# The shared expert's second half and the router: their order in one gated block, on one core

## Chip, cores, metric

One core of one Trainium2 chip. The metric is the device time of one execution in microseconds, as the median of several. TensorE does matrix products, VectorE and ScalarE elementwise work, GpSimd (POOL in the profile) elementwise work more slowly, SyncE (SP) issues DMAs.

## The reference

A gated block on x (8 x 56 tokens of 256): cross attention of 16 heads to 8 contexts of 1500 rows, with fake int8 quantisation on both outer products, then a mixture of 16 experts, two a token, and a shared expert. Only the second part is touched:

```python
x = x + tanh(g_xattn[0]) * xattn(layernorm(x), ctx_2048, ...)
xt = layernorm(x).reshape(-1, D)                      # T = 448 tokens, D = 256
logits = xt @ gate_w.T                                # E = 16
scores = sqrt(softplus(logits))
_, idx = top_k(scores + gate_b, 2)
w = take_along_axis(scores, idx, 1); w = w / w.sum(1, keepdims=True)
pos = position of each (token, choice) among its expert's; valid = pos < CAP   # CAP = 128
buf = zeros((E, CAP, D)).at[e, posc].add(x_pairs)
h = silu(buf @ W1.T) * (buf @ W3.T)                   # I = 176 hidden rows
y = combine(h @ W2.T, w * valid)
shared = (silu(xt @ Ws1.T) * (xt @ Ws3.T)) @ Ws2.T
out = x + tanh(g_ffn[0]) * (y + shared)
```

## The kernel before, in words

Every engine has one list of instructions, written out by hand in its own block; engines meet by semaphores only, and `need(engine, name, n)` is a wait for a count. An engine works its list in order, so where a step stands in the list matters as much as what it waits for.

Attention takes the first 300 us (64 slots, `pe_slot`, `act_slot`, `dve_slot`). Then the attention's output is quantised, projected (L1217) and added (L871), and normalised again (`normalise`, L691, into `xn`, tiles 0 to 2 and then tile 3; tiles are of 112 tokens). The standard deviations come from GpSimd (L445).

From there the second part. Numbers of float32 are carried as two float16 halves: a high half, which ScalarE rounds, and a low half, the difference. A product of two such numbers is three float16 products (`split3`). ScalarE makes the high halves: `xT16[:, 0]` from the turned tokens (L597), `x16[:, :, 0]` from the tokens (L608), `hT[:, 0]` from the shared expert's hidden rows (L611), `w2T` and `w13T` from the weights (`w2_hi` L517, `w13_hi` L523). VectorE makes the low halves of the turned tokens (L876, L878), of the shared hidden rows (L927), and of `w13T` (`w13_lo`, L842). GpSimd makes the low half of `x16` (L448) and of `w2T` (`w2_lo`: a scaling, L436, which waits only for the weight's load, then a subtraction, L439, which waits for `w2_hi`).

TensorE turns the tokens (L1233, L1237), forms the logits in bank 3 (L1243), then the shared expert's gates and ups of four tiles (L1254, banks 2, 4, 5, 7). VectorE copies the logits (L883) and computes softplus from them by a series (L885 to L898) with ScalarE's exp and sqrt (L599, L606), then the two selections (the loop at L912, five steps L914 to L918 each). Between them stand the shared expert's products: `hidden(p)` (L903, L905) makes gate times up of tiles 2p and 2p+1. TensorE turns these into `h_bank` (L1261), ScalarE and VectorE split them (L611, L927), and TensorE multiplies by the shared second weights (L1276), tiles 0 and 1 (p = 0) and 2 and 3 (p = 1). Between the two p stand the places: from `sel16` (the choices, cast at L924) TensorE counts each choice's place (L1268), VectorE finishes `place` (L937, L938).

`place` is turned (L1333), copied by ScalarE (L645) and sent by SP to memory and back as rows (L339 to L343); SP's later weight loads stand behind these. VectorE also compares it to slot numbers (`select`, L946). With this 0/1 matrix TensorE gathers an expert's tokens (`gather`, L1286), ScalarE copies them (`tokens_hi`, L618), TensorE forms gates and ups (`gates_and_ups`, L1303, logged at L1018 in `split3`), ScalarE and VectorE the hidden rows (L628, L973, L977), TensorE turns them (`turn_hidden`, L1310), forms results (L1318, also logged at L1018) and adds them to the tokens in banks 0 and 1 (`add`, L1327). The loop over the 16 experts runs this one expert ahead.

Of the kernel before, what the change touches and what calls it, by code (L numbers as in the profile page):

```python
# [99 lines left out]
def program(nc, x, ctx, cols, rows, gate, wq, wkv, wp, W13, W2, out):  # L100
    stack = ExitStack()
    with stack:
# [129 lines left out]
        def bank16(b):  # L232
# [8 lines left out]
            shared_gu shared_tanh shared_h shared_ht shared_hh shared_hl shared_y xh_done xl_done x16_ready place_turned place_copied place_out place_in0 place_in1 w2_scaled  # L241
# [26 lines left out]
        g_bank = (2, 4, 5, 7)  # L268
        h_bank = (3, 6)
        place_bank = 2  # L270
# [81 lines left out]
        def _(gp):  # L352
# [94 lines left out]
            gp.wait_ge(s["act_post"], 4)  # L447
            gp.tensor_tensor(x16[:, :, 1], xn[:], x16[:, :, 0], ALU.subtract).then_inc(s["x16_ready"], 1)  # L448
# [6 lines left out]
        def _(act):  # L455
# [136 lines left out]
            act.activation(xqT[:, :, 3 * TP:T], bank16(4)[:, 0:NH * TP].rearrange("p (h t) -> p h t", h=NH), ACT.Copy).then_inc(s["oqc_done"], 1)  # L592
            turned = (PS[:, 0:NH, 0:3 * TP], PS[:, 5, 0:NH * TP].rearrange("p (h t) -> p h t", h=NH))
            for k, part in enumerate((slice(0, 3 * TP), slice(3 * TP, T))):
                act.wait_ge(s["lnt_done"], k + 1)
                act.activation(xT[:, :, part], turned[k], ACT.Copy).then_inc(s["lnc_done"], 1)
                act.activation(xT16[:, 0, :, part], turned[k], ACT.Copy).then_inc(s["xh_done"], 1)  # L597
            act.wait_ge(s["dve_post"], 3)
# [9 lines left out]
            act.activation(x16[:, :, 0], xn[:], ACT.Copy).then_inc(s["act_post"], 1)  # L608
            for p in range(2):
                act.wait_ge(s["shared_ht"], p + 1)  # L610
                act.activation(hT[:, 0, p, :], PS[0:IH, h_bank[p], 0:4 * TP], ACT.Copy).then_inc(s["shared_hh"], 1)  # L611
            w2_hi(1)
            w13_hi(1)
# [28 lines left out]

            act.wait_ge(s["shared_y"], 2)
            act.wait_ge(s["place_turned"], 1)
            act.activation(placeT[:], PS[0:E * TT, turn_bank, 0:TP], ACT.Copy).then_inc(s["place_copied"], 1)  # L645
            tokens_hi(0)
# [8 lines left out]
        def _(dve):  # L655
# [217 lines left out]
            for k, part in enumerate(groups):  # L873
                normalise(x1, xn, range(part.start, part.stop), 2 + k).then_inc(s["ln_done"], 1)
            dve.wait_ge(s["xh_done"], 1)
# [4 lines left out]

            logit, e_, z, z2, acc, a, b_, c_ = (r[0], r[1], r[2], r[3], r[4], r[5], r[6], r[7])
# [30 lines left out]
            for k, oh in enumerate((e_, z)):  # L912

                one(dve.tensor_reduce(rs[0][:], bias[:], AX.X, ALU.max))  # L914
                one(dve.tensor_tensor(a[:], bias[:], rs[0][:].unsqueeze(2).to_broadcast([TP, TT, E]), ALU.is_ge))
                one(dve.tensor_tensor(a[:], a[:], rank[:], ALU.mult))
                one(dve.tensor_reduce(rs[0][:], a[:], AX.X, ALU.max))
                one(dve.tensor_tensor(oh[:], a[:], rs[0][:].unsqueeze(2).to_broadcast([TP, TT, E]), ALU.is_equal))  # L918
                if k == 0:
                    one(dve.scalar_tensor_tensor(bias[:], oh[:], -3e38, bias[:], ALU.mult, ALU.add))  # L920
                    hidden(1)
                if k == 1:
                    one(dve.tensor_tensor(c_[:], e_[:], z[:], ALU.add))
                    post(dve.tensor_copy(sel16[:], c_[:]))  # L924

                dve.wait_ge(s["shared_hh"], k + 1)
                dve.tensor_tensor(hT[:, 1, k, :], PS[0:IH, h_bank[k], 0:4 * TP], hT[:, 0, k, :], ALU.subtract).then_inc(s["shared_hl"], 1)  # L927

            one(dve.tensor_tensor(a[:], sc[:], c_[:], ALU.mult))
# [9 lines left out]
            dve.wait_ge(s["act_post"], 3)  # L939
            d.did(dve.tensor_scalar(tgf[:], tg[:, 1:2], 1.0 / FS, None, ALU.mult))  # L940
            d.settle()

# [52 lines left out]
            select(0)  # L995
            select(1)
            w13_lo(1)
            slot_weights(0)
            hidden_rows(0)
# [11 lines left out]
        def _(pe):  # L1011
# [239 lines left out]
            for t in range(TT):  # L1251
                if t == 3:
                    need(pe, "dve_post", 1)
                split3(PS[0:TP, g_bank[t], 0:2 * I], lambda a, h: xT16[:, a, h, t * TP:(t + 1) * TP],  # L1254
                       lambda a, h: w13T[0][:, a, h, :]).then_inc(s["shared_gu"], 1)
            for p in range(2):
                pe.wait_ge(s["shared_h"], 2 * p + 2)
                pe.wait_ge(s["dve_post"], 2)
# [4 lines left out]
            for p in range(2):  # L1263
                if p == 1:
                    pe.wait_ge(s["dve_post"], 4)
                    for t in range(TT):
                        for k in range(t + 1):
                            last = mm(PS[0:TP, place_bank, t * E:(t + 1) * E], (before16 if k == t else ones16)[:], sel16[:, k, :],  # L1268
                                      start=k == 0, stop=k == t)
                    last.then_inc(s["pe_post"], 1)  # L1270
# [7 lines left out]
                last.then_inc(s["shared_y"], 1)  # L1278
            def gather(e):
# [53 lines left out]
            tp(PS[0:E * TT, turn_bank, 0:TP], place[:], ident[0:TP, 0:TP]).then_inc(s["place_turned"], 1)  # L1333
            gather(0)
            weigh_slots(0)
            gates_and_ups(0)
            for e in range(E):
# [63 lines left out]
```

## Time and profile before

| | us |
|---|---|
| median of 3 runs | 416.7 (414.03, 416.7, 418.24) |
| the profiled execution | 412.87 |
| its span, first to last instruction | 411.0 |
| mean granted clock of TensorE | 0.948 |

| engine | busy us | share |
|---|---|---|
| TensorE | 361.2 | 88% |
| VectorE | 304.3 | 74% |
| ScalarE | 250.6 | 61% |
| GpSimd | 124.2 | 30% |

Every time in a row is from the start of the span. A timeline row has the start, the duration, the engine, the line and the operation with its shapes; in brackets the engine's idle time before it and the instruction that ended it. A row may stand for several instructions (x2). The granted clock is a share of full speed, 2.4 GHz: 0.50 is 1.2 GHz.

### The profile page before, as it was taken

The numbers are of one execution on the slowest core, as the hardware profiler recorded it, in microseconds if no ns is written. First come the engines' busy times: TensorE is split into PE (matmuls) and PEld (weight loads), VectorE is DVE, ScalarE is ACT, GpSimd is POOL, SyncE is SP. The second block draws the span as 40 slices with busy tenths as digits, with TensorE's granted clock in tenths as the row PEclk, the third lists the DMA queues.
The fourth block names the chain that finished last, engine by engine and source line by source line (L and its number), as shares of the span: only waits on it lengthen the run. The fifth ranks groups of instructions, "written<-read, shape, count | busy, mean of one in ns | idle before, by whom it ended". The sixth has DMA issues, their size and how long they took to land.

```text
span 411.0 us, 14015 instructions
## 1 busy us (share of the span) xinstructions
PE 361.2 (88%) x5793; PEld 270.3 (66%) x5793; DVE 304.3 (74%) x656; ACT 250.6 (61%) x412; POOL 124.2 (30%) x116
## 2 busy tenths in 40 slices
PE   0996899999999998998999999997853789999993
PEld 0672468568658676766856866874642677888882
DVE  3889885866775775776586676667787786999993
ACT  3574567767776686676776766566532425766661
POOL 6151642222132022122222200010101063777870
PEclk9999799999999999999999999999895757999998
DMA  8969983663474284186163146560000008645001
GB/s 252 192 166 207 208 202 78 106 170 106 76 165 100 81 171 123 51 147 181 54 101 92 39 73 119 146 186 31 3 2 2 0 2 275 196 133 155 8 0 45
DMA packets 34512, 45.65 MB, mean 111 GB/s; under 512 B 3995, under 2 KB 30299, under 8 KB 34323
## 3 DMA queue, kind: packets, MB, share of 16 engines
q1 hardware_dynamic: 33395, 43.74, 44.5%
q0 software_dynamic: 640, 0.78, 1.0%
q8 instruction: 46, 0.75, 0.8%
q10 hardware_dynamic: 416, 0.26, 0.3%
q14 instruction: 15, 0.12, 0.1%
HBM read 25.08 MB, written 0.47 MB: 62 GB/s over the span
## 4 chain that ended last, share of the span: by engine, by line
PE 77%; DVE 13%; issue 4%; ACT 2%; POOL 1%; DMA 1%; DVEq 0%; ACTq 0%; POOLq 0%
PE PS L1018 36%; PE PS L1061 9%; PE PS L1084 9%; PE PS L1095 9%; PE PS L1327 4%; PE PS L1286 3%; DVE mx L777 2%; PE PS L1071 2%; PE PS L1310 2%; DMA x_in<-x 1%; PE PS L1243 1%; DVE KN L726 1%; DVE st L680 1%; PE PS L1276 1%; DVE mtop L781 1%
## 5 line engine op out<-in xcount | busy, mean ns | idle before, releaser
L777 DVE TENSOR_REDUCE mx<-PS 112x1 f32<-112x500 f32 (+1 forms) x128 | 114.4, 933 | 58.5 <-PE PS L1061 58.5
L491 ACT ACTIVATE PT_all<-PS 128x1344 f32<-128x1344 f32 x64 | 82.5, 1289 | 9.2 <-PE PS L1084 9.1
L1018 PE MATMUL PS<-cT,wkvT 128*128 128x500 f16 x288 | 71.5, 385 | 17.7 <-POOL zero L392 11.3
L1018 PE MATMUL PS<-wkvT,cT 128*125 128x256 f16 x576 | 72.8, 278 | 0.5 <-issue 0.5
L1018 PEld LDWEIGHTS PS<-wkvT,cT 128*125 128x125 f16 x576 | 64.9, 139 | 5.9 <-issue 1.1
L385 POOL TENSOR_TENSOR cT<-c_in,cT 128x1000 f16<-128x1000 f32 x18 | 37.5, 2084 | 87.3 <-ACT cT L469 87.3
L1018 PEld LDWEIGHTS PS<-cT,wkvT 128*128 128x128 f16 x288 | 27.5, 99 | 50.5 <-POOL zero L392 11.2
L476 ACT ACTIVATE KN<-PS,col_in 128x500 f16<-128x500 f32 x48 | 32.5, 677 | 40.7 <-PE PS L1018 40.7
L1061 PE MATMUL PS<-arena,QC 96*112 96x500 f16 x192 | 53.1, 384 | 3.1 <-issue 3.1
L1084 PE MATMUL PS<-QC,arena 98*128 98x112 f16 x768 | 49.2, 214 | 3.3 <-ACT QC L511 3.2
L483 ACT ACTIVATE V<-PS 125x512 f32<-125x512 f32 x48 | 28.7, 597 | 31.4 <-PE PS L1018 31.4
L1084 PEld LDWEIGHTS PS<-QC,arena 98*128 98x128 f16 x768 | 41.5, 99 | 9.6 <-ACT QC L511 4.1
L1095 PE MATMUL PS<-PT_all,V 125*17 125x56 f32 x3072 | 45.7, 215 | 1.7 <-ACT PT_all L491 1.6
L726 DVE SCALAR_TENSOR_TENSOR KN<-PS,col_in,KN 128x500 f16<-128x500 f32 x48 | 35.3, 736 | 12.0 <-ACT KN L476 11.2
L1095 PEld LDWEIGHTS PS<-PT_all,V 125*17 125x17 f32 x3072 | 40.3, 99 | 4.1 <-ACT PT_all L491 3.0
L439 POOL TENSOR_TENSOR arena<-arena 88x512 f16<-88x512 f32 x17 | 24.8, 1459 | 34.8 <-ACT arena L517 34.7
L1018 PE MATMUL PS<-arena 88*128 88x256 f16 (+2 forms) x216 | 33.5, 307 | 0.8 <-ACT arena L618 0.7
L409 POOL TENSOR_TENSOR QC<-q,par 96x448 f16<-96x448 f16 x16 | 15.2, 952 | 57.4 <-PE PS L1084 55.6
L1018 PEld LDWEIGHTS PS<-arena 88*128 88x128 f16 (+2 forms) x216 | 22.6, 106 | 9.2 <-issue 1.2
L1061 PEld LDWEIGHTS PS<-arena,QC 96*112 96x112 f16 x192 | 20.5, 133 | 9.9 <-issue 4.2
L469 ACT ACTIVATE cT<-c_in 128x1000 f16<-128x1000 f32 x24 | 24.9, 1036 | 1.8 <-DMA c_in<-ctx 1.4
L1071 PEld LDWEIGHTS PS<-ident,nm 112*2 112x2 f16 x64 | 5.1, 79 | 22.2 <-issue 17.0
(205 smaller groups left out, 449.7 us busy)
## 6 DMA issues: line engine op xcount, KB each, us to landing
arena<-KN SPq DMA_DIRECT2D x144, 125.0 KB, 3.6
c_in<-ctx SPq DMA_DIRECT2D x24, 500.0 KB, 4.6
cT<-W SPq DMA_DIRECT2D x11, 352.0 KB
c_in<-W SPq DMA_DIRECT2D x6, 352.0 KB
cT<-W SPq DMA_DIRECT2D x11, 176.0 KB
arena<-place_far SPq DMA_DIRECT2D x1, 1568.0 KB, 10.3
c_in<-W SPq DMA_DIRECT2D x6, 176.0 KB
PT_all<-L_xattn_wkv SPq DMA_DIRECT2D x1, 512.0 KB, 6.1
```

The costliest lines, as they stand in the source:

```text
L385: gp.tensor_tensor(cT[:, n % 2, 1, :, c * CW:(c + 1) * CW], c_in[:, :, c * CW:(c + 1) * CW], cT[:, n % 2, 0, :, c * CW:(c + 1) * CW], ALU. ...
L439: gp.tensor_tensor(w2T[j % 2][:, 1], w2_s, w2T[j % 2][:, 0], ALU.subtract).then_inc(s["w2l_done"], 1)
L469: act.activation(cT[:, n % 2, 0, :, c * CW:(c + 1) * CW], c_in[:, :, c * CW:(c + 1) * CW], ACT.Copy).then_inc(s["th_done"], 1)
L476: act.activation(KN[:, oh, c, 0, :], PS[:, BANK["K", n, u], 0:CW], ACT.Identity, bias=bk_c[:, oh:oh + 1]).then_inc(s["kh_done"], 1)
L483: act.activation(V[:, n % 2, 2 * v:2 * v + 2, :, 0:DH], PS[0:KP, BANK["V", n, v], :].rearrange("p (t h j) -> p t h j", t=2, h=H), ACT.Copy ...
L491: act.activation(PT_all[:, u % 4, :].rearrange("p (c k) -> p c k", c=CH), PS[:, 3:6, 0:4 * TP], ACT.Exp, scale=SCORE).then_inc(s["exp_done ...
L726: dve.scalar_tensor_tensor(KN[:, oh, c, 1, :], PS[:, BANK["K", n, u], 0:CW], bk_c[:, oh:oh + 1], KN[:, oh, c, 0, :], ALU.add, ALU.subtract ...
L777: dve.tensor_reduce(mx[:, u % 2, k:k + 1], PS[0:TP, k:1 + k * (CH - 1), 0:CW], AX.XY, ALU.max).then_inc(s["red_done"], 1)
L1018: ins = mm(out_, w(a, h), x_(b, h), start=first and k == 0, stop=last and k == len(todo) - 1)
L1061: mm(PS[0:TP, c, 0:CW], QC[0:QR, b % 2, i * TP:(i + 1) * TP], KS[0:QR, b % 2, i, c * CW:(c + 1) * CW], start=True, stop=True).then_inc(s[" ...
L1084: last = mm(PS[:, 3 + t // 4, (t % 4) * TP:(t % 4 + 1) * TP], KS[0:QR + 2, b % 2, i, t * KP:t * KP + 128], QC[0:QR + 2, b % 2, i * TP:(i + ...
L1095: last = mm(PS[32 * j:32 * j + VW, bank, 0:S], V[:, b % 2, t, 4 * hg + j, :], PT[:, (2 * g + j // 2) % 4, t * TP + (j % 2) * S:t * TP + (j ...
```

## The change

- VectorE: `hidden(1)` leaves the loop of the two selections and comes between `select(0)` and `select(1)`. The low halves of the shared hidden rows leave the loop as `shared_lo(p)`: 0 comes behind both selections, 1 behind `slot_weights(0)`. The scale `tgf` comes behind that. `w13_lo(1)` moves from behind `select(1)` to ahead of the low halves of the turned tokens. The low half of `x16` moves from GpSimd to VectorE, ahead of the logits' copy.
- ScalarE: `w2_hi(1)` and `w13_hi(1)` move ahead of the second layer norm's work; the high half of `x16` is made in two parts around the turned tokens' copies, with a semaphore of its own. The shared hidden rows' copy 0 stays, copy 1 comes behind `tokens_hi(0)`; the copy of `place` no longer waits for `shared_y`; that wait stands ahead of `w2_hi(2)`.
- TensorE: turn 0, places, results 0; then the turn of `place`, gather and slot weights of expert 0, turn 1, gates and ups of expert 0, results 1.
- Banks: the shared gates use 2, 6, 4, 3 (the fourth waits for the logits' copy), both turns use bank 5, `place` is turned into bank 6.

```diff
@@ -238,7 +238,7 @@
             oq_done oqt_done oqc_done proj_done ln_done lnt_done lnc_done
-            shared_gu shared_tanh shared_h shared_ht shared_hh shared_hl shared_y xh_done xl_done x16_ready place_turned place_copied place_out place_in0 place_in1 w2_scaled
+            shared_gu shared_tanh shared_h shared_ht shared_hh shared_hl shared_y xh_done xl_done x16h_done x16_ready place_turned place_copied place_out place_in0 place_in1 w2_scaled
             w2h_done w2l_done w13h_done w13l_done
@@ -265,9 +265,9 @@
         proj_at = ((2, 0), (2, D), (1, 0), (3, 0))
-        g_bank = (2, 4, 5, 7)
-        h_bank = (3, 6)
-        place_bank = 2
+        g_bank = (2, 6, 4, 3)
+        h_bank = (5, 5)
+        place_bank, place_t_bank = 2, 6
         gather_bank, gu_bank, turn_bank, y_bank, sum_bank = 2, 3, 4, 5, 7
@@ -444,8 +444,6 @@
-            gp.wait_ge(s["act_post"], 4)
-            gp.tensor_tensor(x16[:, :, 1], xn[:], x16[:, :, 0], ALU.subtract).then_inc(s["x16_ready"], 1)
             for j in range(1, E + 1):
@@ -590,11 +588,21 @@
             act.activation(xqT[:, :, 3 * TP:T], bank16(4)[:, 0:NH * TP].rearrange("p (h t) -> p h t", h=NH), ACT.Copy).then_inc(s["oqc_done"], 1)
+            w2_hi(1)
+            w13_hi(1)
+            def x16_hi(k, part):
+                act.wait_ge(s["ln_done"], k + 1)
+                act.activation(x16[:, part, 0], xn[:, part], ACT.Copy).then_inc(s["x16h_done"], 1)
+            x16_hi(0, groups[0])
             turned = (PS[:, 0:NH, 0:3 * TP], PS[:, 5, 0:NH * TP].rearrange("p (h t) -> p h t", h=NH))
...
                 act.activation(xT16[:, 0, :, part], turned[k], ACT.Copy).then_inc(s["xh_done"], 1)
+            x16_hi(1, groups[1])
             act.wait_ge(s["dve_post"], 3)
@@ -605,12 +613,13 @@
             act.activation(tg[:, 1:2], gx[:, 1:2], ACT.Tanh).then_inc(s["act_post"], 1)
-            act.activation(x16[:, :, 0], xn[:], ACT.Copy).then_inc(s["act_post"], 1)
-            for p in range(2):
+            def shared_hi(p):
                 act.wait_ge(s["shared_ht"], p + 1)
                 act.activation(hT[:, 0, p, :], PS[0:IH, h_bank[p], 0:4 * TP], ACT.Copy).then_inc(s["shared_hh"], 1)
-            w2_hi(1)
-            w13_hi(1)
+            shared_hi(0)
@@ -640,10 +649,11 @@
+            act.wait_ge(s["place_turned"], 1)
+            act.activation(placeT[:], PS[0:E * TT, place_t_bank, 0:TP], ACT.Copy).then_inc(s["place_copied"], 1)
+            tokens_hi(0)
+            shared_hi(1)
             act.wait_ge(s["shared_y"], 2)
-            act.wait_ge(s["place_turned"], 1)
-            act.activation(placeT[:], PS[0:E * TT, turn_bank, 0:TP], ACT.Copy).then_inc(s["place_copied"], 1)
-            tokens_hi(0)
             w2_hi(2)
@@ -872,12 +882,15 @@
                 normalise(x1, xn, range(part.start, part.stop), 2 + k).then_inc(s["ln_done"], 1)
+            w13_lo(1)
             dve.wait_ge(s["xh_done"], 1)
...
+            dve.wait_ge(s["x16h_done"], 2)
+            dve.tensor_tensor(x16[:, :, 1], xn[:], x16[:, :, 0], ALU.subtract).then_inc(s["x16_ready"], 1)
             logit, e_, z, z2, acc, a, b_, c_ = (r[0], r[1], r[2], r[3], r[4], r[5], r[6], r[7])
@@ -918,14 +931,16 @@
                     one(dve.scalar_tensor_tensor(bias[:], oh[:], -3e38, bias[:], ALU.mult, ALU.add))
-                    hidden(1)
                 if k == 1:
...
-                dve.wait_ge(s["shared_hh"], k + 1)
-                dve.tensor_tensor(hT[:, 1, k, :], PS[0:IH, h_bank[k], 0:4 * TP], hT[:, 0, k, :], ALU.subtract).then_inc(s["shared_hl"], 1)
+            def shared_lo(p):
+                dve.wait_ge(s["shared_hh"], p + 1)
+                dve.tensor_tensor(hT[:, 1, p, :], PS[0:IH, h_bank[p], 0:4 * TP], hT[:, 0, p, :], ALU.subtract).then_inc(s["shared_hl"], 1)
+            shared_lo(0)
             one(dve.tensor_tensor(a[:], sc[:], c_[:], ALU.mult))
@@ -936,10 +951,6 @@
             post(dve.tensor_scalar(place[:].rearrange("p (e t) -> p t e", t=TT), b_[:], -1.0, None, ALU.add))
-            dve.wait_ge(s["act_post"], 3)
-            d.did(dve.tensor_scalar(tgf[:], tg[:, 1:2], 1.0 / FS, None, ALU.mult))
-            d.settle()
             def select(e):
@@ -993,9 +1004,13 @@
             select(0)
+            hidden(1)
             select(1)
-            w13_lo(1)
             slot_weights(0)
+            shared_lo(1)
+            dve.wait_ge(s["act_post"], 3)
+            d.did(dve.tensor_scalar(tgf[:], tg[:, 1:2], 1.0 / FS, None, ALU.mult))
+            d.settle()
             hidden_rows(0)
@@ -1250,24 +1265,21 @@
                 if t == 3:
-                    need(pe, "dve_post", 1)
+                    need(pe, "dve_post", 2)
                 split3(PS[0:TP, g_bank[t], 0:2 * I], lambda a, h: xT16[:, a, h, t * TP:(t + 1) * TP],
                        lambda a, h: w13T[0][:, a, h, :]).then_inc(s["shared_gu"], 1)
-            for p in range(2):
+            def turn_shared(p):
                 pe.wait_ge(s["shared_h"], 2 * p + 2)
-                pe.wait_ge(s["dve_post"], 2)
+                need(pe, "shared_hl", p)
                 for k in range(2):
...
                 last.then_inc(s["shared_ht"], 1)
-            for p in range(2):
-                if p == 1:
-                    pe.wait_ge(s["dve_post"], 4)
-                    for t in range(TT):
-                        for k in range(t + 1):
-                            last = mm(PS[0:TP, place_bank, t * E:(t + 1) * E], (before16 if k == t else ones16)[:], sel16[:, k, :],
-                                      start=k == 0, stop=k == t)
-                    last.then_inc(s["pe_post"], 1)
+            def shared_results(p):
                 pe.wait_ge(s["shared_hl"], p + 1)
@@ -1276,6 +1288,15 @@
                 last.then_inc(s["shared_y"], 1)
+            turn_shared(0)
+            pe.wait_ge(s["dve_post"], 4)
+            for t in range(TT):
+                for k in range(t + 1):
+                    last = mm(PS[0:TP, place_bank, t * E:(t + 1) * E], (before16 if k == t else ones16)[:], sel16[:, k, :],
+                              start=k == 0, stop=k == t)
+            last.then_inc(s["pe_post"], 1)
+            shared_results(0)
             def gather(e):
@@ -1330,10 +1351,12 @@
             pe.wait_ge(s["dve_post"], 5)
-            tp(PS[0:E * TT, turn_bank, 0:TP], place[:], ident[0:TP, 0:TP]).then_inc(s["place_turned"], 1)
+            tp(PS[0:E * TT, place_t_bank, 0:TP], place[:], ident[0:TP, 0:TP]).then_inc(s["place_turned"], 1)
             gather(0)
             weigh_slots(0)
+            turn_shared(1)
             gates_and_ups(0)
+            shared_results(1)
             for e in range(E):
```

## Rows read from the trace of the kernel before

**Rows 1.** The chain of waits, 332 to 360 us (start, us, what).
```profile
332.95 0.20 DVE sel L924
333.20 1.11 PE PS L1268 x10
...
337.13 1.72 PE PS L1286 x16
...
343.33 0.49 PE PS L1310 x2
...
359.95 1.55 PE PS L1018 x12
```

**Rows 2.** TensorE's timeline, where it had been idle.
```profile
329.80 0.58 PE L1261 MATMUL PS<-ident,PT_all 112*88 112x112 f32 x4 [2.57 <-DVE PT_all L905]
330.33 2.69 PE L1276 MATMUL PS<-arena 88*112 88x256 f16 x12
...
339.62 1.92 PE L1018 MATMUL PS<-arena 128*128 128x352 f16 x6 [0.69 <-ACT arena L618]
```

**Rows 3.** Windows: us, PE, PEld, DVE, ACT, POOL busy, PEclk, DMA share, GB/s.
```profile
330.50:331.00 0.50, 0.50 (x4) 0.50 (x4) 0.50 (x1) 0.50 (x2) 0.50 (x1) 0.50 0.00 0
...
344.00:344.50 0.50, 0.50 (x4) 0.29 (x5) 0.23 (x1) 0.24 (x1) 0.00 (x0) 0.86 1.07 426
```

**Rows 4.** VectorE's timeline, 317 to 343 us.
```profile
317.96 0.86 DVE L876 TENSOR_TENSOR arena<-qT,arena 128x672 f16<-128x672 f32 x1 [2.54 <-ACT arena L597]
318.73 0.38 DVE L878 TENSOR_TENSOR arena<-qT,arena 128x224 f16<-128x224 f32 x1
320.56 0.22 DVE L883 COPY r<-PS 112x64 f32<-112x64 f32 x1 [1.44 <-PE PS L1243]
...
327.01 0.23 DVE L915 TENSOR_TENSOR r<-r,rs 112x64 f32<-112x64 f32 x1
...
328.30 0.34 DVE L903 SCALAR_TENSOR_TENSOR PT_all<-PT_all,PS 112x176 f32<-112x176 f32 x1
...
329.67 0.61 DVE L927 TENSOR_TENSOR arena<-PS,arena 88x448 f16<-88x448 f32 x1
...
330.43 1.02 DVE L915 TENSOR_TENSOR r<-r,rs 112x64 f32<-112x64 f32 x1
331.49 0.66 DVE L916 TENSOR_TENSOR r<-r,rank 112x64 f32<-112x64 f32 x1
...
335.66 0.22 DVE L938 TENSOR_SCALAR place<-r 112x64 f32<-112x64 f32 x1
...
342.30 0.40 DVE L977 SCALAR_TENSOR_TENSOR PT_all<-PS,slot_w,PT_all 128x176 f32<-128x176 f32 x1
```

**Rows 5.** GpSimd's timeline, 314 to 334 us.
```profile
314.21 0.65 POOL L445 TENSOR_TENSOR rstd<-var,mhalf 112x1 f32<-112x1 f32 x1 [0.82 <-DVE var L686]
329.25 2.12 POOL L448 TENSOR_TENSOR arena<-xn,arena 112x1024 f16<-112x1024 f32 x1 [14.39 <-ACT arena L608]
331.46 1.49 POOL L436 TENSOR_SCALAR arena<-c_in 88x512 f32<-88x512 f32 x1
333.04 1.15 POOL L439 TENSOR_TENSOR arena<-arena 88x512 f16<-88x512 f32 x1
```

**Rows 6.** ScalarE's timeline, 316 to 342 us.
```profile
316.57 0.73 ACT L596 ACTIVATE qT<-PS 128x672 f32<-128x672 f32 x1 [7.36 <-PE PS L1233]
...
328.12 1.06 ACT L608 ACTIVATE arena<-xn 112x1024 f16<-112x1024 f32 x1
...
339.37 0.62 ACT L517 ACTIVATE arena<-cT 88x512 f16<-88x512 f32 x1
341.57 0.32 ACT L628 ACTIVATE PT_all<-PS 128x176 f32<-128x176 f32 x1 [1.58 <-PE PS L1018]
```

**Rows 7.** Timelines of VectorE and GpSimd in the attention, at 48 us.
```profile
48.13 2.20 DVE L786 SCALAR_TENSOR_TENSOR nm<-mtop,nm 112x1 f16<-112x1 f32 x1
...
47.96 2.35 POOL L426 TENSOR_TENSOR x<-x_in,row_in 112x1024 f32<-112x1024 f32 x1
```

## The prediction

> **What bounds the kernel now.** I read the chain of waits first, from the second layer norm (314 us) to the end, then the timeline of each engine in 314 to 350, then windows of half a microsecond for the granted clock. The chain shows two regimes. From 343.33, where the first expert's hidden rows are turned [rows 1], the chain lies on TensorE without a break, expert after expert; the last row of [rows 1] is one of 16 equal pieces. Whatever the change gives must therefore be there at 343.33: behind it nothing is edited, and TensorE's list for an expert is the same. Ahead of it, from the logits to the choice's cast (332.95), the chain runs through VectorE's router [rows 1]. From 333.20 on it is TensorE again: places, shared results, gather, gates, one behind the other [rows 1].
>
> So the question is TensorE's gaps between 327.2 (end of the first turn of the shared hidden rows) and 343.33. Its timeline has three: 2.57 us ahead of the second turn, 0.18 ahead of the places, 0.69 ahead of the first expert's gates, which wait for ScalarE's copy of the gathered tokens [rows 2]. Sum 3.44. The work between them is only reordered by the change. It can win these 3.44 and no more, unless the clock moves. The clock is at its lower level, 1.2 GHz, from about 330.5 (0.50 granted; TensorE had mostly idled since 327.2) until about 344.0, where it goes back to 2.4 GHz (0.86 granted in that half microsecond) [rows 3].
>
> **The change, part by part.**
>
> Router without interruptions. Out of VectorE's queue between the two selections go hidden(1), two pairs, and the first difference of the shared hidden rows: 328.30 to 330.28, 1.98 us [rows 4]. The router's steps also lose their stalls: the same line 915 took 0.23 us in the first selection and 1.02 in the second, with the neighbour 916 at 0.66, while GpSimd made the tokens' low half (329.25, 2.12 us) and started the next weight [rows 4, 5]. With that subtraction gone from GpSimd and the weight's work done long before, both take 0.23: 0.79 + 0.43 = 1.2. The cast moves from 332.95 to 329.75, ends at 329.95.
>
> Tokens' low half on VectorE. New ahead of the logits' copy: one subtraction of 1024 columns. Two subtractions of this form took 0.86 us at 672 columns and 0.38 at 224 [rows 4], 1.07 ns a column, so 1.24 us. It starts behind line 878 (318.73 + 0.38 = 319.11) and ends at 320.35; the logits' copy started at 320.56 after 1.44 us idle [rows 4]. It is hidden with 0.2 to spare. Its ScalarE half is split in two; the whole took 1.06 [rows 6], so the part of 768 columns some 0.8, in ScalarE's wait ahead of the turned tokens, which ends at 316.57 [rows 6] and of which some 1.4 us are left when the first three tiles are normalised (VectorE's wait before line 876 begins at 317.96 - 2.54 = 315.42 with the fourth, a piece of 0.3 later); the part of 256 ends at about 318.8, ahead of 319.11. w2_hi(1) and w13_hi(1), 0.6 and 0.8 us each by the like rows, go into the same wait, which was 7.36 long [rows 6]. If that cover were gone they would delay the turned tokens by 1.4 at most.
>
> w13_lo(1), 0.9 us, goes from a place where VectorE waits anyway to that wait of 2.54 us between the normalised tokens and 317.96 [rows 4]: nothing.
>
> GpSimd's earlier work. With w2h_done raised early, GpSimd runs w2_lo(1) and the scaling of w2_lo(2) right behind the second rstd (314.21 + 0.65 = 314.86): 1.49 + 1.15 + 1.49 and two pauses of 0.09 [rows 5], until 319.2. That is beside VectorE's three subtractions, all with two inputs in SBUF, and such steps are what was held. Bounds: nothing, if they miss each other (GpSimd's own subtraction would end at 317.7, before 317.96); and two holds of the size of line 916's (0.43 each) less the 0.2 to spare, some 0.6. I take 0.2, nearer the lower end, since 916 was the only thing a scaling held. The cast then ends at 330.15.
>
> A rule here speaks against the change. The row: on another stretch a VectorE step of one column took 2.20 us beside a GpSimd sum of 2.35 [rows 7]. The Trainium skill, "SBUF — State Buffer", section "SBUF: two separate sides", says that the pair of ports is an exclusive lock: a VectorE step with two SBUF inputs and a GpSimd step that reads SBUF take turns, each for its whole length. The row of 2.20 agrees. But line 916 was free after 0.66 beside a scaling of 1.49 that had started 0.03 before it [rows 4, 5], so for scalings the trace disagrees. By the rule the sum would come out slower; by the rows it does not (second rival).
>
> TensorE, with the durations of this trace. Idle from 327.2 to 330.2: 3.0 us, the lull ends later than before. Places 1.11 [rows 1], to 331.3. shared_results(0) 2.69 [rows 2], to 334.0. It needs shared_hl 1, which follows the cast by 0.6: there. Meanwhile VectorE needed 2.73 us from the end of the cast to the place numbers (333.15 to 335.88 [rows 1, 4]); now at most that, 332.9, then select(0), 0.65. Turn of places 0.2, gather(0) 1.72 [rows 1], slot weights 0.1: 336.0. The second turn, 0.58 [rows 2], to 336.6, stands where the 0.69 gap was: ScalarE's copy of the tokens (0.6) runs beside it. hidden(1) is done by 335.2. Gates 1.92 [rows 2], to 338.5; shared_results(1) 2.69, to 341.2; its shared_hl 2 is there by 337.8. Then gather(1), 1.72 and 0.1, to 343.0.
>
> New wait: ScalarE waits for shared_y 2 at 341.2 with w2_hi(2), hidden_tanh(0) and all that follows queued behind it. 0.62 for w2_hi(2), then 1.13 from the tanh's start to the end of VectorE's product (341.57 to 342.70 [rows 4, 6]): the hidden rows are ready at 342.95. So the turn is released by both at about 342.95 to 343.0 instead of 343.33. The gap sum agrees: 3.44 out, 3.0 in, 0.4 won. GpSimd's w2_lo(2) slips by 1.8 us behind w2_hi(2), to 342.7, five microseconds before results(1) wants it. SP's three DMAs of the places go 3 us sooner, and the weight loads behind them in its queue too; nobody waited for them.
>
> Clock. From 330.2 to 343 TensorE has no gap now, so I expect the return to 2.4 GHz sooner than 344.0. If it comes near 341 it only speeds gather(1), which then waits for the hidden rows (342.95), and the next gates a little: 0.2. Sum: 0.4 + 0.2 = 0.6 faster.
>
> The profiled execution took 412.87 (span 411.0), 3.8 below the median of the three runs, 416.7 (414.03 to 418.24). Forecast 412.3 for a like execution, so 416.1 for the median. The forecast's own spread is 0.1 to 1.0 faster.
>
> **Rivals.**
>
> *One*: the clock returns ahead of the first gates, at about 336.6. The warm price of gates and results together is 1.55 for six matmuls of 352 columns and six of 256 [rows 1], by columns 0.90 and 0.65; twelve of 256 then 1.30. Gates to 337.5, shared_results(1) from 337.8 (its difference) to 339.1, hidden rows at 340.85: 2.5 faster, 414.2. For: no gap ahead of it since 330.2. Against: here TensorE worked from 333.2 to 338.9 without one and the clock stayed at 0.50. Chance 0.25.
>
> *Two*, slower: the shared ports take full turns. w13_lo(1) waits for the scaling (316.45) and runs to 317.35, GpSimd's subtraction to 318.5, line 876 to 319.35, the next scaling to 320.85, line 878 to 321.2, the new subtraction to 322.45. The logits' copy is 1.9 late, not 0.2, and the router, the lull and all behind it with it: -0.6 + 1.7 = 1.1 slower, 417.8. It decides from a delay of 0.8 on. For: the 2.20 and 1.02 rows. Against: the 0.66. Chance 0.12. (It is what the sentence of the Trainium skill's page "SBUF — State Buffer" told above would make of this kernel.)
>
> *Three*: all 3.2 us of the router reach the end, 413.5. That needs TensorE not to be full behind the cast; it is, but for 0.87. Chance 0.07.
>
> *Four*: the longer quiet (327.2 to 331.3 with only small matmuls, 2.57 idle before) lowers the clock in executions where it now survives. Price, cold against half: gates 1.0, two shared results 2.8, two gathers 1.7: 5.5, so 4.9 slower, 421.6. Against: in this trace it falls already. Chance 0.04; 0.02 is for what I have not seen.
>
> **How the numbers follow.** The forecast has 0.5. About 1%, 4.2 us, is what a measurement of this kernel can tell from no change. None of the cases but the fourth moves that far; what is left is the spread of the median itself, some 2 us by the three runs. Rivals one and three are 1.7 and 1.0 us from the bound: a quarter of their 0.32, and 0.04 of the rest, give faster 0.12. Slower is rival four and a little of two: 0.06. Within 1%: 0.82. Range: 412.6 to 418.4, from below rival three to above rival two.
>
> **What would show it.** Right: line 915 at 0.23 twice; the cast 9.2 us behind the logits' copy (12.4 before); TensorE idle 3 us ahead of the places and hardly at all between them and the first turn of hidden rows; experts as far apart as before. The logits' copy right behind the new subtraction, with steps 876 and 878 longer than 0.86 and 0.38, would show the ports. Wrong: an idle stretch of TensorE of over 0.5 us behind gather(1), a clock that stays at 0.50 beyond 344, or one that falls in other places.

## The result and the profile after

17 runs: median 414.09 us (409.93 to 417.18), before 416.88 (414.03 to 418.54) in the same rounds. The ratio is 0.992, 95% interval 0.989 to 0.995. The changed kernel again in a later batch, 12 runs, gave 0.9996 (0.9955 to 1.0036): e12 below. The two intervals lie side by side and do not overlap (0.9948 against 0.9955). So: faster by 0 to 1%, inside the forecast's 1%, and the time lies in the range. The ratios leave out executions more than 1.5% above the fastest of the same kernel; the profiled ones of the change, of e4 and of e5 are such, which is one more reason to compare kernels by a stretch of their traces, as follows.

The profiled execution of the changed kernel took 416.15 us, more than the 412.87 of before. All of that lies ahead of the normalisation. VectorE's normalisation, the last step that both kernels do alike, starts at 314.05 before and at 320.48 after. Only two of the moved ScalarE steps stand ahead of it (`w2_hi(1)`, `w13_hi(1)`), and they did not delay it: in both kernels it starts 5.19 us behind the start of ScalarE's last copy of the attention's turned output. From it to the logits' copy both need 6.51 us; and from the third expert's turn of hidden rows to the end both need 60.4. In all fourteen traces of this study that last figure is 60.38 to 60.41, and the first ranges from 313.66 to 320.48. Most of what differs from run to run is made in the attention. So I compare kernels by **the stretch**: from the logits' copy to the third turn. It is 30.08 us before (320.56 to 350.64, [rows 4] for its start) and 27.01 after (326.99 to 354.00). Its ends, and the normalisation, in VectorE's and TensorE's timelines, before and then after:

```profile
314.05 1.37 DVE L691 TENSOR_SCALAR xn<-x,mv,rstd 112x256 f32<-112x256 f32 x4
350.64 0.42 PE L1310 MATMUL PS<-ident,PT_all 128*88 128x128 f32 x2
```

```profile
320.48 1.66 DVE L701 TENSOR_SCALAR xn<-x,mv,rstd 112x256 f32<-112x256 f32 x4
354.00 0.42 PE L1331 MATMUL PS<-ident,PT_all 128*88 128x128 f32 x2
```

VectorE's timeline after. Lines 887, 889, 896, 928 and 936 are 876, 878, 883, 915 and 924 of [rows 1, 4]:

```profile
324.38 1.14 DVE L887 TENSOR_TENSOR arena<-qT,arena 128x672 f16<-128x672 f32 x1 [1.44 <-ACT arena L604]
325.44 0.38 DVE L889 TENSOR_TENSOR arena<-qT,arena 128x224 f16<-128x224 f32 x1
325.74 1.21 DVE L893 TENSOR_TENSOR arena<-xn,arena 112x1024 f16<-112x1024 f32 x1
326.99 0.22 DVE L896 COPY r<-PS 112x64 f32<-112x64 f32 x1
...
335.08 0.22 DVE L928 TENSOR_TENSOR r<-r,rs 112x64 f32<-112x64 f32 x1
335.34 0.22 DVE L929 TENSOR_TENSOR r<-r,rank 112x64 f32<-112x64 f32 x1
...
336.37 0.19 DVE L936 CAST sel<-r 112x64 f16<-112x64 f32 x1
...
338.61 0.22 DVE L953 TENSOR_SCALAR place<-r 112x64 f32<-112x64 f32 x1
```

The cast comes 9.38 us behind the logits' copy (12.39 before; forecast 9.2). The selection's steps take 0.22 each where they took 1.02 and 0.66. The new subtraction took 1.21 and ended at 326.95, when TensorE's logits ended too: hidden, with nothing to spare. GpSimd's early work shows in the first row, 1.14 for 0.86.

TensorE's timeline after, to set beside [rows 2]:

```profile
336.61 0.22 PE L1296 MATMUL PS<-sel,before 112*112 112x16 f16 x1 [2.95 <-DVE sel L936]
...
337.15 2.56 PE L1288 MATMUL PS<-arena 88*112 88x256 f16 x12
339.50 0.39 PE L1354 MATMUL PS<-ident,place 112*64 112x112 f32 x1
339.69 1.61 PE L1307 MATMUL PS<-arena 112*128 112x128 f16 x16
...
342.08 1.05 PE L1033 MATMUL PS<-arena 128*128 128x352 f16 x6 [0.27 <-ACT arena L627]
343.09 1.52 PE L1288 MATMUL PS<-arena 88*112 88x256 f16 x12
344.45 1.06 PE L1307 MATMUL PS<-arena 112*128 112x128 f16 x16
345.34 0.24 PE L1315 MATMUL PS<-wt,arena 112*128 112x2 f16 x4
346.41 0.42 PE L1331 MATMUL PS<-ident,PT_all 128*88 128x128 f32 x2 [0.83 <-DVE PT_all L988]
347.38 1.73 PE L1033 MATMUL PS<-arena 128*128 128x352 f16 x12 [0.55 <-DVE arena L852]
```

Two rows of before that [rows 2] does not have:

```profile
333.20 0.26 PE L1268 MATMUL PS<-sel,before 112*112 112x16 f16 x1 [0.18 <-DVE sel L924]
334.16 2.79 PE L1276 MATMUL PS<-arena 88*112 88x256 f16 x12
```

The gap ahead of the places is 2.95, as worked out (3.0). But the first gates take 1.05 where they took 1.92, the second shared results 1.52 instead of 2.79, and TensorE then stands idle twice, 0.83 and 0.55 us, for work that stands behind ScalarE's wait for `shared_y`. The windows say why (the columns are those of [rows 3]):

```profile
337.00:337.50 0.50, 0.50 (x9) 0.50 (x8) 0.44 (x3) 0.00 (x0) 0.00 (x0) 0.93 0.00 0
337.50:338.00 0.50, 0.50 (x4) 0.50 (x3) 0.42 (x3) 0.00 (x0) 0.00 (x0) 0.50 0.00 0
340.50:341.00 0.50, 0.50 (x9) 0.50 (x7) 0.48 (x2) 0.00 (x0) 0.00 (x0) 0.65 0.00 0
341.00:341.50 0.50, 0.50 (x13) 0.50 (x11) 0.50 (x2) 0.16 (x1) 0.00 (x0) 1.00 0.10 21
```

The clock fell to 1.2 GHz at 337.4 and was back at 340.8: low for 3.4 us of the stretch. Before, it was low from 330.5 to 344.1, 13.7 us [rows 3]. So the trace after is the case of my first rival: the clock is back ahead of the first gates (342.08).

### The profile page after: what moved, and what is told of

It is laid out like the page before. It is cut to its first block, busy times and chain, and to the rows that moved or that the text cites. A ratio compares the mean times of both kernels' runs of the same rounds, so it can differ in the third digit from the quotient of the medians.

```text
span 414.4 us, 14014 instructions
## 1 busy us (share of the span) xinstructions
PE 359.3 (87%) x5793; PEld 268.6 (65%) x5793; DVE 306.6 (74%) x657; ACT 250.8 (61%) x413; POOL 122.3 (30%) x115
## 4 chain that ended last, share of the span: by engine, by line
PE 76%; DVE 14%; issue 3%; ACT 2%; POOL 1%; DMA 1%; DVEq 0%; ACTq 0%; POOLq 0%
PE PS L1033 36%; PE PS L1076 9%; PE PS L1110 9%; PE PS L1099 9%; PE PS L1348 4%; PE PS L1307 3%; PE PS L1086 2%; DVE mx L787 2%; DVE mtop L791 2%; PE PS L1331 1%; DMA x_in<-x 1%; PE PS L1288 1%; DVE KN L736 1%; PE PS L1258 1%; DVE st L690 1%
## 5 line engine op out<-in xcount | busy, mean ns | idle before, releaser
L1033 PE MATMUL PS<-cT,wkvT 128*128 128x500 f16 x288 | 72.8, 390 | 22.1 <-POOL rank L393 11.3
L1033 PE MATMUL PS<-wkvT,cT 128*125 128x256 f16 x576 | 74.0, 281 | 0.0
L1033 PEld LDWEIGHTS PS<-wkvT,cT 128*125 128x125 f16 x576 | 66.1, 141 | 5.3 <-issue 0.5
L1110 PE MATMUL PS<-PT_all,V 125*17 125x56 f32 x3072 | 46.7, 218 | 1.6 <-ACT PT_all L489 1.6
L736 DVE SCALAR_TENSOR_TENSOR KN<-PS,col_in,KN 128x500 f16<-128x500 f32 x48 | 35.3, 737 | 14.6 <-ACT KN L474 13.9
L1110 PEld LDWEIGHTS PS<-PT_all,V 125*17 125x17 f32 x3072 | 41.3, 101 | 4.1 <-ACT PT_all L489 4.0
```

Source lines behind the costliest of these rows:

```text
L736: dve.scalar_tensor_tensor(KN[:, oh, c, 1, :], PS[:, BANK["K", n, u], 0:CW], bk_c[:, oh:oh + 1], KN[:, oh, c, 0, :], ALU.add, ALU.subtract ...
L1033: ins = mm(out_, w(a, h), x_(b, h), start=first and k == 0, stop=last and k == len(todo) - 1)
L1110: last = mm(PS[32 * j:32 * j + VW, bank, 0:S], V[:, b % 2, t, 4 * hg + j, :], PT[:, (2 * g + j // 2) % 4, t * TP + (j % 2) * S:t * TP + (j ...
```

## The experiments

Three theories. **C**: the order gives the forecast's 0.4 to 0.6, and the rest is the clock, which returns sooner. **R**: the router's 3 us arrive by themselves. **L**, formed after e5: where the clock is high the kernel before waits for the router, so the order is worth more there than where it is low.

All of them in one table. The ratio is to the kernel before on the same chip (5 rounds each; 17 runs for the change, 6 for e2, 12 for the others); cast, stretch and clock are of one trace each. e1 to e4 ran on one chip, e5 to e8 on a second, e9 to e12 on a third; only there does the changed kernel stand beside them, so only e9 to e11 can be compared with it by ratio. "Clock low" is for how long it was at 0.50 again after it had risen in the shared gates, by windows (the rise itself comes 3.0 to 4.9 us behind the logits' copy in all of them).

| kernel | cast behind logits | clock low | stretch | ratio (interval) |
|---|---|---|---|---|
| before | 12.39 | 13.7 | 30.08 | 1 |
| the change | 9.38 | 3.4 | 27.01 | 0.9918 (0.9889 to 0.9948) |
| e12, the change again | 9.30 | 6.8 | 27.98 | 0.9996 (0.9955 to 1.0036) |
| e1, before, filled | 12.69 | 10.2 | 30.43 | 0.9988 (0.9945 to 1.003) |
| e5, before, filled twice | 12.97 | 6.8 | 30.42 | 0.9977 (0.9932 to 1.0022) |
| e9, before, filled thrice | 12.58 | 0 | 28.02 | 0.9967 (0.9926 to 1.0007) |
| e2, the change, filled | 9.58 | 0 | 26.98 | 0.9881 (0.9819 to 0.9942) |
| e3, hidden(1) inside | 10.89 | 6.8 | 29.64 | 0.9969 (0.9934 to 1.0004) |
| e4, x16 late | 11.08 | 10.2 | 31.33 | 1.0006 (0.9958 to 1.0053) |
| e7, before, x16 early | 11.18 | 13.7 | 29.88 | 0.9997 (0.9956 to 1.0038) |
| e8, the change, norm filled | 9.28 | 6.8 | 28.26 | 0.9947 (0.9903 to 0.9991) |
| e6, tanh first | 9.32 | 3.4 | 26.95 | 0.9968 (0.9918 to 1.0017) |
| e10, expert first | 9.51 | 3.4 | 25.99 | 0.9896 (0.9853 to 0.9939) |
| e11, e10 filled | 9.71 | 0 | 25.96 | 0.9905 (0.9861 to 0.9949) |

**e1, e2, e5, e9: matmuls nobody reads, in TensorE's gaps.**

```diff
             for p in range(2):
+                if p == 1:
+                    for _ in range(16):
+                        mm(PS[0:TP, 2, 0:2 * I], xT16[:, 0, 0, 0:TP], w13T[0][:, 0, 0, :], start=True, stop=True)
```

In e1 this stands behind the first turn (the diff), in e2 (18 of them) behind `turn_shared(0)`. e5 has 8 more ahead of the wait for the places, e9 also 5 ahead of the turn of the places, 3 ahead of the gather and 4 ahead of the gates; these 12 go into bank 6.

> The kernel before, with 16 extra matmuls of 352 columns (shared gates' operands, into bank 2, whose content nobody reads any more) behind the first turn of the shared hidden rows, in TensorE's idle 2.57 us. Theory C (the clock): the change's order gives only 0.4 to 0.6 us, and the rest of the 3.4 us measured is TensorE going back to 2.4 GHz some 10 us sooner. Then this kernel, which keeps its clock through 327 to 344, is 3 to 4 us faster than the kernel before, with no reordering at all, and the stretch from the logits' copy to the third expert's turn of hidden rows (30.1 us in the trace of before) comes to 26 to 27. Theory R (the router): the 3.2 us that leave the router's queue arrive at the end by themselves. Then the filling gives 0 to 1 us here, and the stretch stays near 29 to 30.

> The changed kernel with 18 such matmuls behind the first turn, in TensorE's 2.95 us of idle time ahead of the places. Theory C: with the clock at 2.4 GHz in both, only the order is left: 0.4 to 1 us faster than the filled kernel before, and 0 to 1.5 faster than the changed kernel. Theory R: about 3 us faster than the filled kernel before.

> The filled kernel before, with 8 more such matmuls just ahead of the wait for the places, where its trace showed TensorE idle for 1.4 us and the clock back at 1.2 GHz right after. Theory C (the clock is what the change's gain is made of): with the clock at 2.4 GHz through to the experts, the kernel before needs 26 to 27.5 us from the logits' copy to the third expert's turn, as the changed one (27.0), and is 2.5 to 4 us faster than before. Theory R (the 3 us of the router's earlier end arrive by themselves): that stretch stays within 1 us of 30, the cast being as late as before.

> The kernel before, filled twice and now also in its last three gaps: 5 matmuls ahead of the turn of the places, 3 ahead of the gather, 4 between it and the first gates (into bank 6, unread then). In the last trace the clock fell at those gaps and the stretch stayed at 30.4. Theory L (it is the cast that counts wherever the clock is high: there the kernel before waits for the router, and the order is worth the router's 3 us): with the clock held through, this kernel's stretch from the logits' copy to the third turn is 28.5 to 29.5, still 1.5 to 2.5 longer than the changed one's 27.0. Theory C (all of the gain is clock): 26 to 27.5.

e1 did not test what it was meant to: TensorE did the first shared results in 1.52 and then idled again, and the clock went down at 338.9 for 10.2 us. Its stretch did not get shorter. TensorE's timeline of e1:

```profile
334.98 1.52 PE L1279 MATMUL PS<-arena 88*112 88x256 f16 x12
337.88 0.22 PE L1271 MATMUL PS<-sel,before 112*112 112x16 f16 x1 [1.38 <-DVE sel L924]
...
338.42 2.38 PE L1279 MATMUL PS<-arena 88*112 88x256 f16 x12
```

e5 closed that gap. The clock stayed at 2.4 GHz until 343.75, and still the stretch was 30.42. That is outside theory C's 26 to 27.5, but not yet a clean test: at the high clock TensorE only waited more, for the places, for the selection and for ScalarE's copy (0.79, 0.45 and 0.70), and from 343.75 it was at 1.2 GHz again for 6.8 us, the first gates (1.92) within them. TensorE's timeline of e5:

```profile
339.61 1.51 PE L1281 MATMUL PS<-arena 88*112 88x256 f16 x12
341.90 0.26 PE L1338 MATMUL PS<-ident,place 112*64 112x112 f32 x1 [0.79 <-DVE place L938]
342.61 1.07 PE L1291 MATMUL PS<-arena 112*128 112x128 f16 x16 [0.45 <-DVE arena L946]
343.51 0.24 PE L1299 MATMUL PS<-wt,arena 112*128 112x2 f16 x4
344.46 1.92 PE L1018 MATMUL PS<-arena 128*128 128x352 f16 x6 [0.70 <-ACT arena L618]
```

With those three filled too (e9) the clock was high all the way (1.00 from 330 to 348 by windows) and the stretch was 28.02, between what L (28.5 to 29.5) and C (26 to 27.5) had said. TensorE's timeline of e9:

```profile
336.57 0.22 PE L1273 MATMUL PS<-sel,before 112*112 112x16 f16 x1 [0.19 <-DVE sel L924]
339.41 0.26 PE L1340 MATMUL PS<-ident,place 112*64 112x112 f32 x1
...
341.96 1.05 PE L1018 MATMUL PS<-arena 128*128 128x352 f16 x6
...
351.76 0.42 PE L1317 MATMUL PS<-ident,PT_all 128*88 128x128 f32 x2
```

The filling itself held nothing up: the places are turned 0.37 us behind VectorE's last step on them in e9 as in e5, and the gates start 0.74 behind ScalarE's copy (0.75 in e5). e2 holds the changed kernel at the same clock: 26.98. The order alone is thus worth 1.04 us at the high clock, by one trace of each. The kernel before loses 2.06 (30.08 to 28.02) to the low clock, the changed one 0.03 at 3.4 us of it (27.01) and 1.0 to 1.3 at 6.8 (27.98 in e12, 28.26 in e8). Between the changed kernel's trace and before's, 3.07 us, the order makes 1.0 and the clock 2.0. That the clock returned sooner is seen in all seven traces that have the new order and no filling in that gap (low for 3.4 to 10.2 us, against 13.7 in before and e7); why it did is not shown.

**e4, e7: the two halves of the change apart.** e4 is the change with the tokens' halves late again, the high one behind the scale's tanh (the diff); e7 is before with them early, and `w2_hi(1)` and `w13_hi(1)` too.

```diff
+            gp.wait_ge(s["x16h_done"], 2)
+            gp.tensor_tensor(x16[:, :, 1], xn[:], x16[:, :, 0], ALU.subtract).then_inc(s["x16_ready"], 1)
...
-            x16_hi(0, groups[0])
...
-            x16_hi(1, groups[1])
...
+            act.activation(x16[:, :, 0], xn[:], ACT.Copy).then_inc(s["x16h_done"], 2)
...
-            dve.wait_ge(s["x16h_done"], 2)
-            dve.tensor_tensor(x16[:, :, 1], xn[:], x16[:, :, 0], ALU.subtract).then_inc(s["x16_ready"], 1)
```

> The changed kernel with both halves of the tokens back where they were: the high half on ScalarE behind the scale's tanh, the low half on GpSimd behind it. GpSimd's 2.1 us then lie beside the second selection again. Both theories: one of the selection's two-input steps is held, 0.8 to 1.2 us, and the cast comes that much later; 0.8 to 1.5 slower than the changed kernel. If the stalls had another cause, the selection's steps stay at 0.23 and the time is that of the changed kernel.

> The kernel before with only the tokens' halves moved (high half around the turned tokens' copies, low half on VectorE ahead of the logits' copy) and w2_hi(1), w13_hi(1) ahead of the second layer norm. The order of hidden(1), the places and the shared results is that of before. Both theories: the held steps (1.02, 0.66, 0.67) are back at 0.23, the cast comes 1.2 us sooner. Theory R: 1.2 us faster than before. Theory C: TensorE's gaps are 3.4 less 1.2 at most, but it starts the shared results at the same point, which wait for the second turn and not for the cast: 0 to 0.5 faster unless the clock's return moves.

e7 did what both theories had for the cast (1.2 us sooner, no step held) and gained 0.2 in the stretch, nothing in the time: TensorE waited 2.57 us for the same second turn, and worked on at 1.2 GHz. Theory C's 0 to 0.5 is right here, R's 1.2 is not. e4 was worse than foreseen (0.8 to 1.5 slower than the changed kernel): its stretch is 3.4 us longer than e12's, and its places are finished 3.4 us later (15.0 behind the logits' copy, 11.5 in e12). GpSimd's subtraction met the last step ahead of the cast, and its weight work behind it met the arithmetic of the weights and places. VectorE's and GpSimd's timelines of e4:

```profile
335.05 2.02 DVE L934 TENSOR_TENSOR r<-r 112x64 f32<-112x64 f32 x1
337.11 0.62 DVE L935 CAST sel<-r 112x64 f16<-112x64 f32 x1
...
338.90 0.99 DVE L946 TENSOR_TENSOR r<-r,rs 112x64 f32<-112x64 f32 x1
339.92 0.64 DVE L947 CAST wt<-r 112x64 f16<-112x64 f32 x1
...
340.99 0.47 DVE L952 TENSOR_SCALAR place<-r 112x64 f32<-112x64 f32 x1
```

```profile
334.79 2.21 POOL L448 TENSOR_TENSOR arena<-xn,arena 112x1024 f16<-112x1024 f32 x1 [14.46 <-ACT arena L616]
337.08 1.49 POOL L436 TENSOR_SCALAR arena<-c_in 88x512 f32<-88x512 f32 x1
338.66 1.15 POOL L439 TENSOR_TENSOR arena<-arena 88x512 f16<-88x512 f32 x1
339.89 1.49 POOL L436 TENSOR_SCALAR arena<-cT 88x512 f32<-88x512 f32 x1
```

VectorE's 2.02 and 0.99 end 0.07 and 0.08 us behind GpSimd's two subtractions, each held to its end. The casts beside the scalings are held for 0.4 only. So neither half pays alone in the stretch: e7 gains 0.2, e4 loses 1.25 against before, together they gain 2.1 to 3.1. With the router ahead of the shared work each held step is on the path; with the shared work ahead of it, it was not.

**e3: hidden(1) back between the selections.**

```diff
                     one(dve.scalar_tensor_tensor(bias[:], oh[:], -3e38, bias[:], ALU.mult, ALU.add))
+                    hidden(1)
```

> The changed kernel with hidden(1), 1.45 us of VectorE, back between the two selections. Both theories: the cast and the places come 1.45 us later and TensorE idles 4.4 us ahead of them. Theory R: 1.4 to 1.5 slower than the changed kernel. Theory C: 1.4 in the gap, and up to 1 us more if the longer quiet puts the clock's return off; between 1.4 and 2.5 slower.

The cast is 1.5 later, the gap ahead of the places 4.46, the stretch 1.7 longer than e12's at the same 6.8 us of low clock, 2.6 longer than the first trace's. Its ratio, 0.9969, cannot be told from e12's. Both theories had 1.4, so it does not tell them apart; the 1.7 is near that.

**e8: the gap ahead of the turned tokens.**

```diff
                 project_out(k, part)
+            for _ in range(16):
+                mm(PS[0:TP, 6, 0:2 * I], xqT[:, 0, 0:TP], w13T[0][:, 0, 0, :], start=True, stop=True)
```

> The changed kernel with 16 matmuls of 352 columns (attention's turned outputs by w13T[0], into the unread bank 6) behind the last output projection, in TensorE's 5.2 us of idle time ahead of the turned tokens. If the clock counts for what follows: turns, logits and shared gates (1.9, 3.2 and 5.2 us now, nearly all at 1.2 GHz) run at 2.4 GHz, the logits 1 to 1.8 us sooner, and the kernel 1 to 2 us faster than the changed one. If the copies and the router hide it, or if the filling itself delays the turn (16 at 0.29 us is 4.7 of 5.2), 0 to 0.5.

A miss for the most part. The clock came back at 313.8, but went down again at 317.2, during the sixteen logit matmuls of 16 columns each, and up at 324.0, 4.2 us behind the logits' copy, no sooner than in the others. From the normalisation to the logits' copy it took 6.12 instead of 6.51: 0.4 us, where 1 to 1.8 was the hope.

**e6, e10, e11: ScalarE's new wait.** In e6 only the tanh goes ahead of it, in e10 the next gates' high half too (the diff; the loop then leaves it out for e = 0), e11 is e10 with e2's filling.

```diff
+            hidden_tanh(0)
+            w13_hi(2)
             act.wait_ge(s["shared_y"], 2)
             w2_hi(2)
-            hidden_tanh(0)
```

> The changed kernel with ScalarE's first expert's tanh ahead of its wait for shared_y 2 and of w2_hi(2). The traces of the changed kernel and of its filled form both show TensorE idle 0.83 us ahead of the first turn of hidden rows and 0.55 ahead of the next gates, behind that tanh. If this new wait is on the path, as the prediction has it: the tanh 2 us sooner, both gaps gone or small, the stretch 25.6 to 26.3 instead of 27.0, 0.7 to 1.4 us faster than the changed kernel. If it is covered: no change.

> The changed kernel with hidden_tanh(0) and w13_hi(2) ahead of ScalarE's wait for shared_y 2. The last form moved only the tanh: the turn came at 18.4 us behind the logits' copy instead of 19.4, but TensorE then stood 1.53 us for w13_lo(2), whose high half was still behind that wait. With both ahead that gap goes: stretch 25.4 to 26.2 instead of 26.95 to 27.0, 0.8 to 1.5 us faster than the changed kernel. If another wait takes its place (the second expert's tokens, GpSimd's w2_lo(2)): 26.5 to 27.

> The same with 18 matmuls in TensorE's idle 2.95 us ahead of the places. The fill kept the clock high throughout in its first trace, where the stretch was then bound by the waits behind the new shared_y wait. With those gone the high clock should be worth something: stretch 24.8 to 25.8, 0 to 0.8 us faster than without the fill. If VectorE's router sets the end anyway: the same as without.

e6: the turn came 18.4 us behind the logits' copy instead of 19.4, and the whole went into the next wait (1.53): the stretch is 26.95, not the 25.6 to 26.3 foreseen. TensorE's timelines of e6 and of e10:

```profile
338.83 0.40 PE L1331 MATMUL PS<-ident,PT_all 128*88 128x128 f32 x2
340.76 1.73 PE L1033 MATMUL PS<-arena 128*128 128x352 f16 x12 [1.53 <-DVE arena L852]
```

```profile
341.67 0.40 PE L1333 MATMUL PS<-ident,PT_all 128*88 128x128 f32 x2
342.46 1.71 PE L1035 MATMUL PS<-arena 128*128 128x352 f16 x12 [0.39 <-issue]
```

e10 took both away: stretch 25.99 with the same 3.4 us of low clock, 1.02 shorter than the change's, and a median of 412.14 beside 415.05 for the changed kernel on the same chip in the same rounds. The two intervals of that chip do not overlap (0.9853 to 0.9939, 0.9955 to 1.0036); with the first result's, 0.9889 to 0.9948, e10's does. By stretch and by the batch's medians it beats both kernels. e11 is no better: at the high clock throughout the stretch is 25.96, so what is left in it is not TensorE's speed. Beside e9, before at the high clock throughout, that is 2.06 us of the 2.87 by which the cast is earlier.

**e12: the change again.** It was expected to give 0.989 to 0.995, and a stretch of 26.9 to 28.3 with the clock low for 3.4 to 6.8 us. The stretch is 27.98 at 6.8, the ratio 0.9996: the stretch is where it was expected, the ratio is not. Here the clock came back only behind the first gates, which took the low price. TensorE's timeline:

```profile
341.27 1.86 PE L1033 MATMUL PS<-arena 128*128 128x352 f16 x6
342.97 1.48 PE L1288 MATMUL PS<-arena 88*112 88x256 f16 x12
```

The executions that were not traced have one figure each, the mean granted clock of the whole. Its median is 0.955 over the first 17 of the changed kernel and 0.9495 over e12's 12, beside 0.944, 0.945 and 0.948 for the kernel before in the three batches of experiments. The batch with the smaller gain in clock is the one with no gain in time. That fits the clock's share of the gain; it does not prove it, as the attention is in this mean too.

## Why the prediction was right or wrong

- *The router without interruptions*: right. 9.38 for 9.2; the held steps came back to 0.22, and e7 shows the 1.2 us of them alone.
- *The tokens' low half on VectorE*: right, 1.21 for 1.24. The 0.2 for the ports was too much in this trace: step 876 was 0.28 longer, but the logits were not copied later. Rival two did not come. Its mechanism is real, and e4 shows it at 1.8 and 0.8 us; the change takes it off the path instead of onto it.
- *TensorE's gap ahead of the places*: right, 2.95 for 3.0.
- *The new wait behind `shared_y`*: right in place and size (from the end of the shared results, 344.65, to the turn, 346.41, is 1.76 for 1.75), wrong in weight. I had it level with gather(1), which I priced at the low clock. At the high clock it is the end of everything, 0.83 + 0.55 us of idle TensorE. e10 shows 1.0 of it.
- *The clock*: this is the step whose size failed. I gave it 0.2 us, for a return at about 341, and took every matmul of 331 to 341 at the low price. e9 puts 2.06 us on the low clock of the kernel before, and e2 and the changed kernel's trace differ by 0.03. Counted from the logits' copy, the clock fell at 9.9 us before and at 10.4 after, but came back at 13.8 instead of 23.5; I had looked for about 20. In e12 it came back at 17.1. Why it returns at 13.8 in one execution and at 17.1 in another of the same kernel stays open.
- *Where it fell in the end*: 0.6 was forecast, the medians say 2.8 and, in e12's batch, 1.0. Rival one had 2.5 for a return 16 us behind the logits' copy, ahead of the first gates. The first trace of the changed kernel is that case (13.8, stretch 3.1 shorter than before's). e12 is not: its clock returned a little later, with the first gates already done at the low price, and its stretch is 2.1 shorter. That its 2.1 in e12 shows as 0.04% in the time of that batch says how little one batch can tell here. The forecast's own case, a return about 20 us behind the logits' copy, came up in no trace of the changed kernel, so its 0.6 is untested. The bound of 1% held in both batches, the direction only in the first. That the time lies in the range is owed in part to the range's width, 5.8 us, so it is partly luck: what the order gives is 1.0 of the 3.07 us in the stretch, and the larger part is the clock of rival one, to which I had given a chance of 0.25. Rival three needed TensorE with time to spare; at the high clock it has some, and 1.0 of the 3.0 us arrives (2.1 of 2.9 in e11, with the new wait out of the way). Rival four, a clock that falls where it had not, was not seen in two traces of the changed kernel.

## What to carry to other kernels

Before a chain is shortened, ask for both clocks what it is hidden behind: here, in the old order, 1.2 us less of router gave 0.2 with TensorE at 1.2 GHz (e7), while at 2.4 GHz TensorE waited for it (e5), so one trace gives one of two prices. Where runs differ by more than the change is worth, find the last point before and the first point behind it between which the kernels differ, and compare that stretch. A wait that a step moves behind should hold back nothing but its own user: the weight's copy needed `shared_y`, the two instructions queued behind it did not.

## What the runs showed of the hardware

- A GpSimd subtraction held a VectorE step with two inputs in SBUF to its own end (2.02 for 0.23 beside 2.21). A GpSimd scaling of 1.49 held VectorE's casts for only 0.4. The Trainium skill, "SBUF — State Buffer", "SBUF: two separate sides", has whoever starts first keep the pair of ports "for the whole instruction". The two subtractions of e4 agree (VectorE's 2.02 and 0.99 end with them), the scaling does not (step 916 was through after 0.66 beside its 1.49, [rows 4, 5]).
- A full busy row did not keep the clock up: in e8 it fell to 1.2 GHz 0.8 us into the sixteen matmuls of 16 columns. TensorE had stood idle for 0.69 and 0.59 us in the 2.3 us before them; whether those gaps or the short matmuls made it fall is not shown.
- A later fall of the clock made the kernel before no faster: it fell 9.9, 13.9 and 17.9 us behind the logits' copy in before, e1 and e5, and the stretches were 30.08, 30.43 and 30.42. Only with no fall at all (e9) was it 28.02.
- The last 60.4 us of every execution repeat to 0.03. Two traces of one kernel differ by 1.0 in the stretch; the time ahead of the normalisation differs by 6.8 over all traces (e8's filling is behind part of it there, 313.66; without it the least is 313.92).
